# The second round's scatter of a two-round graph network: rows as weights, one-hots streamed

## What is computed

```
h = relu(layernorm(x))
for t in range(2):
    m = concat([h[dst], h[src], edge_weight], axis=1) @ msg_W[t].T + msg_b[t]
    agg = segment_sum(m, src, N)        # one sum per source node
    h = gru_cell(agg, h, Wih[t], bih[t], Whh[t], bhh[t])
out = x + h
```

## Time and profile before

| | |
|---|---|
| median of 3 runs | 2404.67 us |
| lowest and highest run | 2390.03 and 2408.36 us |
| profiled execution, its time | 2394.16 us |
| profiled execution, its span | 2392.5 us |
| busy share: TensorE, VectorE, ScalarE, GpSimd | 68%, 91%, 82%, 26% |
| granted TensorE clock, mean over the span | 0.98 |

### The profile page before, as it was taken

One profiled execution on the slowest core, in us unless ns is written; L12 is line 12 of the kernel. 1 busy time (PEld: TensorE's weight loads), 2 busy tenths in 40 slices (PEclk: granted clock), 3 DMA queues, 4 the chain that ended last, 5 costly groups with the idle time before them and its releaser, 6 DMA issues. The chain is left out here.

```text
span 2392.5 us, 126600 instructions
## 1 busy us (share of the span) xinstructions
PE 1623.6 (68%) x47260; PEld 1526.9 (64%) x47260; DVE 2179.6 (91%) x3727; ACT 1963.7 (82%) x4428; POOL 616.3 (26%) x853
## 2 busy tenths in 40 slices
PE   0000000000139999999999999869999999999996
PEld 0000000000138899999999999868999999999996
DVE  7999999999269899999999999868999999999995
ACT  4777894553158899999999999868999999999996
POOL 1000000000643344554444544301121211112121
PEclk9999999999969999999999999989999999999998
DMA  6100001111427676666677676566777777777773
GB/s 118 28 0 0 0 0 48 35 22 34 113 57 239 211 227 226 227 229 223 231 224 231 226 229 227 167 200 218 236 239 231 237 241 232 235 239 234 234 237 113
DMA packets 175418, 400.70 MB, mean 167 GB/s; under 512 B 73071, under 2 KB 76789, under 8 KB 174855
## 3 DMA queue, kind: packets, MB, share of 16 engines
q1 hardware_dynamic: 116907, 204.17, 27.6%
q0 software_dynamic: 57296, 195.19, 24.7%
q10 hardware_dynamic: 1132, 0.27, 0.1%
HBM read 384.63 MB, written 14.57 MB: 167 GB/s over the span
## 5 line engine op out<-in xcount | busy, mean ns | idle before, releaser
L1202 ACT ACTIVATE rows<-ps_rows 128x512 f16<-128x512 f32 x2744 | 1454.6, 632 | 74.7 <-PE ps_rows L1124 55.5
L1141 PE MATMUL ps_sum<-rows,src 128*64 128x132 f16 (+1 forms) x21952 | 1151.5, 225 | 16.0 <-ACT rows L1202 11.0
L1141 PEld LDWEIGHTS ps_sum<-rows,src 128*64 128x64 f16 x21952 | 903.0, 142 | 29.0 <-ACT rows L1202 20.1
L1296 DVE TENSOR_TENSOR src<-iota_units,src_lane 128x2048 f16<-128x2048 f16 (+1 forms) x784 | 863.4, 1101 | 41.7 <-PE ps_sum L1141 41.6
L1124 PE MATMUL ps_rows<-rows_next,dst 128*64 128x128 f16 x10976 | 546.3, 220 | 37.9 <-DVE dst L1287 21.0
L1124 PE MATMUL ps_rows<-rows_now,dst 128*64 128x128 f16 x10976 | 545.4, 219 | 18.2 <-DVE dst L1287 7.3
L1287 DVE TENSOR_SCALAR dst<-lanes,lane_no 128x2048 f16<-128x2048 f16 (+1 forms) x784 | 533.0, 680 | 10.4 <-DMA lanes<-lanes_dram 10.1
L860 PE MATMUL ps_src<-ident,late 112*64 112x112 f32 x98 | 29.6, 333 | 624.6 <-DVE taken L930 613.0
L1124 PEld LDWEIGHTS ps_rows<-rows_next,dst 128*64 128x64 f16 x10976 | 411.3, 112 | 60.2 <-ACT rows L1202 21.5
L1124 PEld LDWEIGHTS ps_rows<-rows_now,dst 128*64 128x64 f16 x10976 | 412.0, 111 | 41.7 <-issue 12.7
L860 PEld LDWEIGHTS ps_src<-ident,late 112*64 112x64 f32 x98 | 14.1, 143 | 630.2 <-DVE taken L930 614.1
(11 more groups left out here) (188 smaller groups left out, 2039.0 us busy)
## 6 DMA issues: line engine op xcount, KB each, us to landing
lanes<-lanes_dram POOLq DMA_DIRECT2D x294, 512.0 KB, 4.9
lanes<-lanes_dram SPq DMA_DIRECT2D x294, 512.0 KB, 4.7
lanes<-lanes_dram POOLq DMA_DIRECT2D x98, 256.0 KB, 4.2
lanes<-lanes_dram SPq DMA_DIRECT2D x98, 256.0 KB, 4.2
rows_now<-parts_dram SPq DMA_DIRECT2D x112, 32.0 KB, 1.8
rows_next<-parts_dram SPq DMA_DIRECT2D x112, 32.0 KB, 3.8
parts_dram<-rows_now SPq DMA_DIRECT2D x1, 3136.0 KB, 16.2
sorted_dram<-planes SPq DMA_DIRECT2D x1, 3136.0 KB, 11.6
```

Source lines behind the costliest of these rows:

```text
L1141: last = nc.tensor.matmul(ps_sum[b][at, 0:width], hot[:, at], row, start=(j == 0), stop=(j == J - 1))
L1202: nc.scalar.activation(rows[:, (u + NU * b) % ring, 0:n, 0:2 * H], cut(ps_rows[(u + NU * b) % 4][:])[:, 0:n, :], ACT.Copy).then_inc(rows_r ...
L1296: nc.vector.tensor_tensor(src1[q][:, 0:len(units)], iota_units[:].rearrange("p (o l) k -> p o l k", o=1) .broadcast_to([P, len(units), P, ...
```

## The change

Only the second round (`flipped`, r = 1) is changed, with a different layout of its gate weights, which the setup loads.

- *Scatter*: the weights are now 64 columns of `rows` (the high or the low values), and the stream is `src1`, 128 nodes at a step of four elements. So `ps_sum` holds features on partitions and nodes along the columns: high parts on partitions 0 to 63, low parts on 64 to 127.
- *Joining*: ScalarE copies only the low half (64 partitions, scaled by 1/LO) into `sums`; VectorE adds it to the high half, read from PSUM, straight into `turned_now` (features on partitions, as the gates need it).
- *Transposes*: only `copied` and `scaled` are left of four. ScalarE copies 128 columns instead of 256.
- *Extras*: once, at the start of the round, TensorE transposes all nodes' extras (`turn_extras`), ScalarE copies them, SyncE writes them to `extras_dram` and then fetches for each tile its two rows of 128 values into rows 65 and 66 of `turned_now`. VectorE fills the constant row once.
- *Weights*: 13 small DMAs in the setup instead of 8, as the rounds' layouts differ.
- *Tail*: the transposes of the last two tiles stand between the last scatters, ahead of the last sums' copy.

The diff, cut:

```diff
-                    for to, at in ((w_first[0:H, :, 0:G], w_sum[0:H, :, :]),
+                    later = slice(1, ROUNDS)
+                    for to, at in ((w_first[0:H, 0:1, 0:G], w_sum[0:H, 0:1, :]),
...
+                                   (w_first[0:H, later, 0:G], w_node[0:H, later, 4 * H:4 * H + G]),
+                                   (w_second[0:H, later, 0:G], w_sum[0:H, later, :]),
...
-                sp.wait_ge(weights_in, 16 * 8)
+                sp.wait_ge(weights_in, 16 * 13)
...
+                    def fetch_extras(k, b):
+
+                        wait(sp, gates_ready, k - 1)
+                        plain(sp.dma_start(turned_now[b][H + 1:H + 3, P:2 * P],
+                                           extras_dram[bass.ds(k, 1), :, :].rearrange("o v p -> (o v) p"))).then_inc(extras_in[b], 16)
+
                     if not more:
                         def body(s, b, half):
                             fetch_lanes(sp, s)
+                            if not past(s, 1):
+                                sp.wait_ge(extras_kept, 1)
+                                sp.dma_start(extras_dram.rearrange("t v p -> t (v p)"), extras_across[0:NT, :]).then_inc(extras_out, 16)
+                                sp.wait_ge(extras_out, 16)
+                                sp.wait_ge(ones_in, 4)
+                            else:
+                                fetch_extras(s - 1, 1 - b)
...
                         if u == 0:
-                            wait(te, sum_ready, s - 1)
+                            wait(te, joined_ready if flipped else sum_ready, s - 1)
                         for k, j in enumerate(pairs_of(u)):
                             hot = src1[q][:, u - q * UQ, :, k]
                             row = rows[:, (u + NU * b) % ring, k, :]
                             for at in HALVES:
-                                last = nc.tensor.matmul(ps_sum[b][at, 0:width], hot[:, at], row,
-                                                        start=(j == 0), stop=(j == J - 1))
+                                if flipped:
+                                    last = nc.tensor.matmul(ps_sum[b][at, 0:P], row[:, at], hot, start=(j == 0), stop=(j == J - 1))
+                                else:
+                                    last = nc.tensor.matmul(ps_sum[b][at, 0:width], hot[:, at], row,
+                                                            start=(j == 0), stop=(j == J - 1))
...
+                        if flipped:
+                            te.wait_ge(extras_kept, 1)
+                            nc.tensor.matmul(ps_T[high, 0:P], copied[b][:], ident[:], start=True, stop=True)
+                            nc.tensor.matmul(ps_T[low, 0:P], scaled[b][:], ident[:], start=True, stop=True).then_inc(turned, 1)
+                            return
...
+                        if flipped:
+                            te.wait_ge(joined_ready, k + 1)
+                            te.wait_ge(extras_in[b], 16 * half + 16)
...
                     for u in range(NU - LAG, NU):
+                        if flipped and u < NU - LAG + 2:
+                            turn(NT - 2 + u - NU + LAG, u - NU + LAG)
                         scatter(NT - 1, u, (NT - 1) % 2)
...
+                        if flipped:
+                            nc.scalar.activation(sums[b][:], ps_sum[b][P - H:P, 0:P], ACT.Copy, scale=1.0 / LO).then_inc(sum_ready, 1)
+                            return
...
-                        nc.scalar.activation(turned_now[b][:], ps_T[:, 0:2 * P], ACT.Copy).then_inc(T_ready, 1)
+                        n = P if flipped else 2 * P
+                        nc.scalar.activation(turned_now[b][:, 0:n], ps_T[:, 0:n], ACT.Copy).then_inc(T_ready, 1)
...
+                        if flipped:
+                            wait(dve, turned, k - 1)
+                            plain(nc.vector.tensor_scalar(scaled[b][:], h[:, bass.ds(k, 1), 0:H].rearrange("p o f -> p (o f)"),
+                                                          both[:, 1:2], None, ALU.mult)).then_inc(scaled_ready, 1)
+                            dve.wait_ge(sum_ready, k + 1)
+                            wait(dve, gates_ready, k - 1)
+                            nc.vector.tensor_tensor(turned_now[b][0:H, P:2 * P], sums[b][:], ps_sum[b][0:H, 0:P],
+                                                    ALU.add).then_inc(joined_ready, 1)
+                            return
```

More of the change, by code:

```diff
@@ L970, in sums_round @@
         def sums_round(r, scope):
-            copied, extras, scaled, turned_now = [[sb(f"{name}{b}", [P, n], scope=scope) for b in range(2)] for name, n in
-                                          (("copied", H), ("extras", H), ("scaled", H), ("turned_now", 2 * P))]
+            copied, scaled, turned_now = [[sb(f"{name}{b}", [P, n], scope=scope) for b in range(2)] for name, n in
+                                          (("copied", H), ("scaled", H), ("turned_now", 2 * P))]
+            if r == 0:
+                extras = [sb(f"extras{b}", [P, H], scope=scope) for b in range(2)]
+            else:
+                extras_across = sb("extras_across", [P, 2 * P], scope=scope)
             rz, tn, cand = [sb(name, [P, 2, n], scope=scope) for name, n in (("rz", 2 * H), ("tn", H), ("cand", H))]
@@ L980, in sums_round @@
             more = r + 1 < ROUNDS
+            flipped = r > 0
             ring = NU if r == 0 else 4
@@ L991, in sums_round @@
             ps_rows = [ps(f"ps_rows{b}", [P, 512], scope=scope) for b in range(4)]
-            sums = [sb(f"sums{b}", [P, width], scope=scope) for b in range(2)]
-            joined = [sb(f"joined{b}", [P, H], scope=scope) for b in range(2)]
+            if flipped:
+                sums = [sb(f"sums{b}", [H, P], scope=scope) for b in range(2)]
+            else:
+                sums = [sb(f"sums{b}", [P, width], scope=scope) for b in range(2)]
+                joined = [sb(f"joined{b}", [P, H], scope=scope) for b in range(2)]
             ps_sum = [ps(f"ps_sum{b}", [P, 512], scope=scope) for b in range(2)]
@@ L1002, in sums_round @@
              extras_zero, extras_ready, scaled_ready, copied_ready, turned, T_ready, gates_ready,
-             rz_ready, tn_ready, cand_ready, mixed, h_new, ones_ready, joined_ready) = [path_sem(f"{n}_{r}") if more or n not in ("attr_sum", "ones_ready", "rows_zero") else None for n in names]
+             rz_ready, tn_ready, cand_ready, mixed, h_new, ones_ready, joined_ready) = [path_sem(f"{n}_{r}") if not flipped or n not in ("attr_sum", "ones_ready", "rows_zero", "extras_zero", "extras_ready") else None for n in names]
             lanes_in = [path_sem(f"lanes_in{r}_{q}") for q in range(NQ)]
+            extras_turned, extras_kept, extras_out, ones_in = [path_sem(f"{n}_{r}") if flipped else None
+                                                               for n in ("extras_turned", "extras_kept", "extras_out", "ones_in")]
+            extras_in = [path_sem(f"extras_in{r}_{b}") for b in range(2)] if flipped else None
             new_high = path_sem(f"new_high{r}") if more else None
@@ L1031, in body @@
                             fetch_lanes(sp, s)
+                            if not past(s, 1):
[3 more added lines that the diff above has]
+                                sp.wait_ge(ones_in, 4)
+                            else:
+                                fetch_extras(s - 1, 1 - b)
                         in_pairs(sp, NT, body, DEEP)
+                        fetch_extras(NT - 1, (NT - 1) % 2)
+                        for b in range(2):
+                            sp.wait_ge(extras_in[b], 16 * (NT // 2))
                         return
@@ L1173, in _, with turn_extras @@
                         te.wait_ge(rows_zero, 1)
+                    def turn_extras():
+                        for v in range(2):
+                            last = nc.tensor.transpose(ps_T[0:NT, v * P:(v + 1) * P], edge_sums[:, :, v], ident[:])
+                        last.then_inc(extras_turned, 1)
                     def body(s, b, half):
@@ L1178, in body @@
                             gather(s, u, b)
+                            if flipped and not later_tile and u == TURN_AT:
+                                turn_extras()
                             if u >= LAG:
@@ L1249, in body @@
                             take(s, u, b)
+                            if flipped and not one_back and u == TURN_AT + 1:
+                                take_extras()
                             if one_back and u == SUM_AT:
@@ L1346, in left_over @@
                                                       ALU.subtract)).then_inc(new_left, 1)
[L1348 to L1353, removed]
+                    if flipped:
+                        for b in range(2):
+                            nc.vector.memset(turned_now[b][H:P, P:2 * P], 0.0).then_inc(ones_in, 1)
+                        dve.wait_ge(ones_in, 2)
+                        for b in range(2):
```

(9 more changed lines are left out.)

31 lines of the change are left out of this document (22 added, 9 removed).

## The result

The changed kernel takes 2653.44 us (median of 6 runs, 2650.69 to 2665.37) against 2400.15 us before (6 runs). The ratio is 1.107, with a 95% interval of 1.103 to 1.110: slower by a tenth. The forecast was 2618 us, slower.

The account below looks back on a forecast made before the run. TensorE alone was to bound the second round: 4.42 us more in each of 49 periods is 217; 2394.2 + 217 + 2 = 2613, said as 2618 us with part of the median's offset; 8-in-10 range 2366 to 2690.

Parts of the forecast that it names:

- The step that decided it: Second-round scatter: streaming every fourth element takes 0.43 us per eight matmuls at full clock, adding 5.32 us a period.
- The first rival: Second-round scatter: the step is free for the stream, 0.22 us per eight; ScalarE bounds, 2372 to 2374 us; chance 0.20.
- The second rival: Second-round scatter: the step costs the stream half of a load's price, 0.33 us per eight; 2474 us; chance 0.08.
- The third: Second round, TensorE: granted clock falls because the array is fed at half pace; 28.4 us a period, 2997 us; chance 0.02.
- One of my witnesses: Slot stage: f32 weight loads, 110 ns packed and 138 ns at an 8-byte step, agree that the step costs time.
- The smaller signs: Second round: scatter loads fall to 111 ns, gathers keep 0.22 us, ScalarE and VectorE fall to some 76% busy.
- The period: Second round, two node tiles: 16.10 + 5.32 - 0.44 - 0.46 = 20.52 us, bound by TensorE, 49 times.
- the single costs: Once per run: first-tile wait +2, setup DMAs +1, transposes at the end -1; together +2 us.
- SyncE's queue: Second round, each tile: the added extras DMA delays nothing; without its cover 0.2 us a tile or 20 us in all.
- Its hold in the first tile: Second round's start: SyncE holds tile 1's lanes until the extras are written to DRAM; 0 to 4 us, taken as +2.
- The 13 weight DMAs: Setup: 13 weight DMAs for 8 put SyncE 3.3 us ahead of the window loads; 0 to +2 us, say +1.
- My cover of 4 us: Setup: the last window load is issued at 591.70 us, VectorE's sort ends at 595.71.

Follow-up runs that it names:

- the packed stream: The changed kernel, its second-round scatter streaming 128 neighbouring f16 elements of src1 instead of every fourth: 2373.49 us, ratio 0.991.
- the run with packed weights: The kernel before, its second-round scatter weights taken from 64 neighbouring elements of src1: 2380.03 us, ratio 0.992.
- the step of two: The changed kernel, its second-round scatter streaming every second element of src1 instead of every fourth: 2367.32 us, ratio 0.989.
- a step of three: The changed kernel, its second-round scatter streaming every third element of src1 instead of every fourth: 2496.28 us, ratio 1.040.
- The weight load at a step of eight: The kernel before, its second-round scatter weights read at every eighth element of src1: 2675.23 us, ratio 1.115.

## Why the prediction was right

**The step that decided it held.** I priced the stream by the weight loads that read at the same step, and took it to keep the pace of half clock: 0.43 us per eight scatters, between 0.22 and 0.46. It was 0.447. The wording was too wide: the loads that read at this step do speed up with the clock, from 177 to 141 ns, only by less than the packed ones. What keeps its pace is the reading part, and the stream shows it alone, with 0.46 us at half clock and 0.447 at full. The first rival (a free step) falls with the changed kernel. What I worked out for it, a kernel bound by ScalarE at 2372 to 2374 us, is what the packed stream measured (2373), but partly by luck: the period was 15.40 us and not 15.66, 13 us less in the round, and the round's first 20 tiles took 16 us more than ten such periods, of which the kernel before has 7 too. The second rival (half the price) falls with 0.447; it would have been 0.33. The third (a lower clock) falls with the clock of 1.00 in the middle of the round.

**One of my witnesses was no witness.** I read the f32 loads of the earlier trace rows, 110 ns packed and 138 at an 8-byte step, as a second sign of the step's cost. The same trace has f32 weights of 64 neighbouring elements in the second round, `joined`, at the same length:

```profile
L1153 PEld LDWEIGHTS ps_T<-ident,joined 128*64 128x64 f32 x150 | 15.0, 139 | 0.0
```

So 138 ns in an f32 load need no step. That the f16 load's 141 ns came from the step rests on the run with packed weights, where they fell to 110.

**The smaller signs.** The scatter's loads fell to 119 ns, not 111. The gathers went to 0.24 us, where I had said that they keep 0.22. VectorE fell to 72% busy and ScalarE to 82%, where I had said some 76% for both.

**The Trainium skill's rule** (Advanced Engine Details and Errata, Memory Cachelines) is wrong for TensorE at full clock in the number of hits, two. Two hits on a line cost twice, at step 4 (112 ns a couple for 56), and four are nearly free, at step 2 (59). At half clock two are nearly enough: 0.46 us for 0.43. Its lines of 16 bytes fit the table, which does not show them.

**The sum came out 39 us low** (2613 for the profiled execution, which took 2652.1).
- *The period* was forecast at 20.52 us and is 21.48, worth +47 us in 49 periods. Eight scatters take 0.204 us more than before where I had added 0.19: 0.4 us a period. Eight gathers take 0.240 instead of 0.22, 0.6 us a period: I had held them constant, without a row for it. Transposes and gates are within 0.02.
- *The first tiles* gave 9 us back. From the first gather of the round to the last the kernel before took 795.7 us, 7 more than 49 x 16.10: its first 20 tiles took 168.4 us for 161. The changed kernel took 1050.7, 2 less than 49 x 21.48. I had scaled the whole round by its middle.
- *The rest* is 1 us: the round began 4.3 us later and its tail is 1.3 us shorter, with +2 forecast for the single costs.

**One cover held, one did not.** SyncE's queue: no engine waited for the extras' rows in the middle of the round. Its hold in the first tile is there; SyncE's queue at the start of the round, and VectorE's wait for lanes from 1570 to 1700 us:

```profile
1580.23 0.42 SPq L1058 DMA_DIRECT2D extras_dram<-extras_across  x1
...
1582.03 2.44 SPq L1036 DMA_DIRECT2D lanes<-lanes_dram  x4
...
DVE dst L1355 <- DMA lanes<-lanes_dram: 7.7, 3, 3.8
```

The wait was 4.4 us before, so the hold cost VectorE 3.3 us (+2 forecast), but TensorE, now the bound, did not wait for it. In the step of two, where TensorE is faster, it waited 2.06 us for VectorE's `dst1` before the gather at 1582.44.

The 13 weight DMAs did cost something. In the setup the window loads have to be in before SyncE goes on, and all engines meet at the end of that block. The last window loads and the next instruction of VectorE, changed kernel, then the latter before:

```profile
598.76 1.83 SPq L636 DMA_DIRECT2D rows_now<-parts_dram  x2
602.61 0.15 DVE L899 TENSOR_SCALAR own_start<-lane_no 128x1 f32<-128x1 f32 x1 [3.19 <-PEq L597]
...
596.04 0.15 DVE L892 TENSOR_SCALAR own_start<-lane_no 128x1 f32<-128x1 f32 x1 [0.33 <-PEq L596]
```

The last window load was issued by 600.59 us, behind the end of VectorE's sort at 599.41, so VectorE stood still for 3.19 us instead of 0.33: 2.9 us, where I gave 0 to +2. All six kernels with the 13 DMAs show 1.7 to 3.2 us there, all four with 8 show 0.33. My cover of 4 us was the gap between issue and sort, and left out that the loads must also land.

The first gather of the round stands at 1577.1 us in the changed kernel and at 1572.8 before. Of these 4.3 us, 2.9 are that wait, and 0.9 lie between the last gather of the first round and the first of the second (28.7 us, 27.8 before; 28.1 to 29.4 in all kernels with the swap, 27.4 to 27.8 in all without). The remainder varies from run to run: VectorE's sort ended 3.7 us later, and the first round, which the change leaves alone, took 3.2 us less. In the experiments the first gather stands anywhere from 1571.9 (the step of two, which has all of the change) to 1583.4.

## What to carry to other kernels

Before an operand of a matmul is moved from the weights to the stream, look at its innermost step: count the 16-byte pieces that its elements touch, at some 1.7 ns each for 128 elements of f16, against 0.44 ns per column (56 ns for 128). Here a load at a step of four elements was hidden behind the matmuls but for 4 ns a couple, and one at a step of eight was not; the stream at a step of four was not hidden at all, and twice as many elements pass there. Rows at half clock tell such a read apart: what takes equally long at both clocks does not go by the array's clock. A layout chosen for one engine (four interleaved pairs, for VectorE) may be halved at no cost to it, as it was here (1221 ns for 1228). And when a queue gets more to issue, count its cover up to the landing of the last transfer and not up to its issue.

## What was not expected

- The kernel before already paid for its layout: packing the weights of one round gained 0.8% (0.992), by 141 to 110 ns a load and 0.24 to 0.22 us per eight scatters, where TensorE and ScalarE stood within 2% of each other.
- A read at a step of three costs by the piece too (87 ns), in between the neighbours (59 and 112); nothing is rounded up to powers of two.
- Eight gathers behind a stream at a step of four or eight take 0.24 us and not 0.22, though behind a step of three they take 0.23. Their loads are 117 ns instead of 110 or 111. No run here tells why.
- The weight load at a step of eight took 209 ns, 68 more than at a step of four for 32 more pieces, 2.1 ns each against 1.7 for the stream. That is open too.
- The faster kernels lose in the first 20 tiles of the second round what they don't lose later: the packed stream took 169.7 us for them, 16 more than ten of its later periods of 15.40. Why was not tried.
